# Attention on one core: value bursts of two key tiles side by side, maxima six ahead, and the maxima's turn in the sums' bank

## The reference, cut to what matters

```python
q = (query @ Wq).reshape(b, sq, 32, 32).transpose(0, 2, 1, 3)   # 32 heads of 32
k = (key @ Wk).reshape(b, sk, 8, 32).transpose(0, 2, 1, 3)      # 8 key/value heads, 4 query heads each
v = (value @ Wv).reshape(b, sk, 8, 32).transpose(0, 2, 1, 3)
scores = jnp.einsum('bhqd,bhkd->bhqk', q, jnp.repeat(k, 4, axis=1)) * 32 ** -0.5
probs = jax.nn.softmax(scores, axis=-1)
out = jnp.einsum('bhqk,bhkd->bhqd', probs, jnp.repeat(v, 4, axis=1))
```

## Time and profile before

| | |
|---|---|
| median of 3 runs (lowest to highest) | 915.27 us (914.51 to 922.08) |
| the profiled execution | 919.78 us, span 918.0 us |
| attention, first score of group 0 to the last value burst | 346.7 to 773.9 us of the span |
| PE busy over the span | 846.3 us, 92% |
| DVE, ACT, POOL busy | 591.5, 448.6, 534.0 us |
| costliest groups | reductions 301.0 us (x256), exponentials 279.7 us (x512), scores 179.8 us (x512), items' matmuls 156.3 us (x512), value bursts 137.5 us (x1024) |

### The profile page before, as it was taken

How to read it: one execution, slowest core, us unless ns; L and a number is a source line. 1 busy time by engine, 2 the same in 40 slices (tenths; PEclk the granted TensorE clock), 3 DMA queues, 4 the chain that set the end, 5 groups by cost and what they waited for, 6 DMA issues and landing times.

```text
span 918.0 us, 13982 instructions
## 1 busy us (share of the span) xinstructions
PE 846.3 (92%) x4456; PEld 333.9 (36%) x4456; DVE 591.5 (64%) x846; ACT 448.6 (49%) x741; POOL 534.0 (58%) x235
## 2 busy tenths in 40 slices
PE   3789898969979999999999999999999988999998
PEld 2656564424424442222222222222222212444443
DVE  4657545988836756777876777787877731254621
ACT  4244435645521216666666667677676665021200
POOL 3544125974623334778878888888888788122100
PEclk9799899989989999999999999999999999999999
DMA  6899884322997521554454455445544433222232
GB/s 206 231 211 230 197 216 92 89 84 47 150 229 199 148 73 44 125 124 91 99 105 95 107 123 112 95 100 109 123 93 108 92 69 70 46 48 57 57 126 80
DMA packets 121673, 107.80 MB, mean 117 GB/s; under 512 B 86176, under 2 KB 106656, under 8 KB 117536
## 3 DMA queue, kind: packets, MB, share of 16 engines
q1 hardware_dynamic: 116160, 73.69, 31.8%
q0 software_dynamic: 4608, 33.56, 18.1%
q10 hardware_dynamic: 864, 0.00, 0.0%
HBM read 41.55 MB, written 12.58 MB: 59 GB/s over the span
## 4 chain that ended last, share of the span: by engine, by line
PE 60%; DVE 14%; DMA 7%; issue 7%; SPq 4%; DVEq 4%; ACT 2%; POOLq 1%; POOL 0%; ACTq 0%
PE sbank L1564 10%; PE sbank L1573 10%; PE mpair L1504 9%; DVE mx L1268 5%; DVEq L931 4%; PE sbank L1642 3%; PE sbank L1657 3%; PE sbank L1646 3%; PE sbank L1659 3%; PE sbank L1644 3%; PE sbank L1403 3%; PE sbank L1404 3%; PE sbank L1405 3%; DMA regD<-mT 2%; PE sbank L1583 2%
## 5 line engine op out<-in xcount | busy, mean ns | idle before, releaser
L1268 DVE TENSOR_REDUCE mx<-mpair 128x1 f32<-128x1024 f32 x256 | 301.0, 1215 | 86.6 <-PE mpair L1504 86.4
L873 ACT ACTIVATE regC<-sbank 128x512 f32<-128x512 f32 x512 | 279.7, 595 | 127.3 <-PE sbank L1564 126.6
L1564 PE MATMUL sbank<-regD 98*128 98x512 f16 x512 | 179.8, 388 | 11.9 <-DMA regD<-mT 6.0
L603 POOL TENSOR_TENSOR wraw<-regC 128x2048 f32<-128x2048 f32 x32 | 145.2, 4537 | 25.8 <-ACT regC L873 14.9
L1504 PE MATMUL mpair<-regD 96*128 96x512 f16 x512 | 156.3, 382 | 3.8 <-DVE mT L1278 3.5
L1573 PE MATMUL sbank<-regC,regD 128*32 128x512 f32 x1024 | 137.5, 609 | 1.0 <-ACT regC L873 1.0
L1564 PEld LDWEIGHTS sbank<-regD 98*128 98x128 f16 x512 | 46.3, 97 | 204.6 <-ACT regC L873 164.8
L603 POOL TENSOR_TENSOR regD<-regC 128x2048 f32<-128x2048 f32 x16 | 72.7, 4541 | 27.9 <-ACT regC L873 27.9
L603 POOL TENSOR_TENSOR tail<-regC 128x2048 f32<-128x2048 f32 x16 | 76.7, 4791 | 0.8 <-ACT regC L873 0.8
L1504 PEld LDWEIGHTS mpair<-regD 96*128 96x128 f16 x512 | 49.2, 99 | 55.7 <-DVE mT L1278 10.6
L496 POOL TENSOR_SCALAR xT_lo<-xT_lo,sc 128x1024 f32<-128x1024 f32 x16 | 29.5, 1846 | 65.9 <-DVE X L977 46.9
(11 more groups left out here) (170 smaller groups left out, 1264.9 us busy)
## 6 DMA issues: line engine op xcount, KB each, us to landing
regD<-wraw POOLq DMA_DIRECT2D x16, 1024.0 KB, 7.0
tail<-wraw POOLq DMA_DIRECT2D x16, 1024.0 KB, 7.0
xT_lo<-in_ctx SPq DMA_DIRECT2D x16, 512.0 KB, 5.1
wraw<-in_L_ffn_W_int SPq DMA_DIRECT2D x8, 512.0 KB, 4.4
X<-in_x SPq DMA_DIRECT2D x4, 1024.0 KB, 8.0
wraw<-in_L_xattn_Wq SPq DMA_DIRECT2D x8, 512.0 KB, 3.8
wraw<-in_L_xattn_Wo SPq DMA_DIRECT2D x8, 512.0 KB, 4.5
regD<-q_hi_scratch SPq DMA_DIRECT2D x32, 128.0 KB, 2.4
```

The costliest lines, as they stand in the source:

```text
L603: nc.gpsimd.tensor_tensor(p_sum[pr if pr < 3 else 1][:, :, :], probs[:, (2 * pr) % 4, :, :], probs[:, (2 * pr) % 4 + 1, :, :], ALU.add).th ...
L873: nc.scalar.activation(probs[:, kt % 4, h, :], bank[4 + h % 2], ACT.Exp, scale=SCALE).then_inc(s["exp_ok"], 1)
L1268: v.tensor_reduce(mx[m][:, bass.ds(n, 1)] if par is not None else mx[m][:, n:n + 1], slot[:, :, :], AX.XY, ALU.max).then_inc(s["mx_red"], 1)
L1564: pe.matmul(bank[4 + h % 2], kst[par][0:98, kt * P:(kt + 1) * P], qst[par][0:98, h * 512:(h + 1) * 512], start=True, stop=True).then_inc(s ...
```

## The change

`att` on PE goes through 4 pairs of key tiles, a and b, instead of 8 tiles. Scores 0 and 1 of a pair's first tile stand at the end of the pair before (of the first pair, at its start). Then come the value bursts of both tiles of the pair before, back to back, in pairs 0 and 2 followed by `sum_half`. Behind them, S for a score and M for half of an item: S(a2) M S(a3) M S(b0) M M S(b1) S(b2) M M S(b3) M S(next a0) M S(next a1). So a pair has the same 8 scores and 8 halves of 4 items as two tiles had.

`LEAD` is 6. Pair 0 takes items 6 to 9 of the next group, pair 1 items 10 to 13, pair 2 items 14 and 15 and then 0 and 1 of the group after, pair 3 items 2 to 5. The query projections take two more items (3 + 3 instead of 2 + 2), and the group before the last two fewer. `turn_max` stands directly behind the value bursts of pair 3, and writes into bank 7 instead of bank 2, so nothing in `mpair1` waits for `split_max` any more; it waits instead until bank 7 has been read (`inv_ok`). On DVE `invert`'s second part moves behind item 15, and `split_max` behind the reduction of item 0 of the group after. ACT, POOL and SP keep their instructions and order.

```diff
-        LEAD = 4
+        LEAD = 6
...
-        Q1_ITEMS += [[(0, ITEMS - 1)]] + [[(1, 2 * n), (1, 2 * n + 1)] for n in range(LEAD // 2)]
+        Q1_ITEMS += [[(0, ITEMS - 1)]] + [[(1, 3 * n + i) for i in range(3)] for n in range(LEAD // 3)]
...
                     if not first and n == ITEMS - 3:
                         invert(g - 1, 0)
-                        invert(g - 1, 1)
-                if ahead >= 1:
-                    split_max(g + 1, cur, g // 3 + 1)
+                if not first:
+                    invert(g - 1, 1)
                 for n in range(LEAD):
                     if ahead >= 2:
                         reduce_item(g + 2, far, n)
+                    if n == 0 and ahead >= 1:
+                        split_max(g + 1, cur, g // 3 + 1)
...
             def turn_max(g, par):
                 pe.wait_ge(s["mx_red"], ITEMS * (g + 1))
-                pe.transpose(bank[2][:, 0:P], mx[par][:, :], id32[:, :]).then_inc(s["mt_mm"], 1)
+                if not (isinstance(g, int) and g < 2):
+                    pe.wait_ge(s["inv_ok"], g - 1)
+                pe.transpose(bank[7][:, 0:P], mx[par][:, :], id32[:, :]).then_inc(s["mt_mm"], 1)
...
+                def half_pair(i, half):
+                    if i < len(items):
+                        dg, par, n = items[i]
+                        if half == 0:
+                            pe.wait_ge(s["mx_red"], ITEMS * (g + dg) + n - 1)
+                        max_half(par, n, n % 2, half)
+
+                pe.wait_ge(mrow[cur], 32 * (g // 3 + 1))
+                for j in range(NPAIR):
+                    ka, kb = 2 * j, 2 * j + 1
+                    if j == 0:
+                        score(g, cur, ka, 0, first)
+                        score(g, cur, ka, 1, first)
+                        if not first:
+                            pv(g - 1, far, KT - 2)
+                            pv(g - 1, far, KT - 1)
+                    else:
+                        pv(g, cur, ka - 2, first)
+                        pv(g, cur, ka - 1, first)
+                    if j in (0, 2) and not first:
+                        sum_half(g - 1, j // 2, isinstance(g, int) and g == 1)
+                    if j == 2 and ahead >= 2:
+                        pe.wait_ge(stg[far], 112 * ((g + 2) // 3 + 1))
+                    if j == 3 and ahead >= 1:
+                        turn_max(g + 1, nxt)
+                    items = [todo.pop(0) for _ in range(4) if todo]
+                    score(g, cur, ka, 2, first)
+                    half_pair(0, 0)
+                    score(g, cur, ka, 3, first)
+                    half_pair(0, 1)
+                    score(g, cur, kb, 0, first)
+                    half_pair(1, 0)
+                    half_pair(1, 1)
+                    score(g, cur, kb, 1, first)
+                    score(g, cur, kb, 2, first)
+                    half_pair(2, 0)
+                    half_pair(2, 1)
+                    score(g, cur, kb, 3, first)
+                    half_pair(3, 0)
+                    if j < NPAIR - 1:
+                        score(g, cur, kb + 1, 0, first)
+                    half_pair(3, 1)
+                    if j < NPAIR - 1:
+                        score(g, cur, kb + 1, 1, first)
```

More of the change, by code:

```diff
@@ L1275, in split_max @@
                     dve.wait_ge(mrow[prev], 32 * nth_prev)
-                v.tensor_scalar(mT[0][:, :], bank[2][0:16, 0:P], -1.0 / MROW, None, ALU.mult)
+                v.tensor_scalar(mT[0][:, :], bank[7][0:16, 0:P], -1.0 / MROW, None, ALU.mult)
                 d()
-                v.scalar_tensor_tensor(out=mT[1][:, :], in0=bank[2][0:16, 0:P], scalar=-1.0 / MROW, in1=mT[0][:, :],
+                v.scalar_tensor_tensor(out=mT[1][:, :], in0=bank[7][0:16, 0:P], scalar=-1.0 / MROW, in1=mT[0][:, :],
                                        op0=ALU.mult, op1=ALU.subtract).then_inc(s["mt_cp"], 1)
@@ L1540, in between @@
                     if j == 3 and len(items) > 1:
-                        if items[-1] == (1, 1):
-                            pe.wait_ge(s["mt_cp"], 1)
                         max_scores(*items[-1][:1], *items[-1])
@@ L1591, in att @@
                 todo += [(2, far, n) for n in range(LEAD)] if ahead >= 2 else []
[L1593 to L1596, removed]
-                        turn_max(g + 1, nxt)
[L1598 to L1621, removed]
+                def half_pair(i, half):
[4 more added lines that the diff above has]
+                        max_half(par, n, n % 2, half)
@@ L1634, in _ @@
             att(G - 1, 0, ahead=0)
+            pv(G - 1, 0, KT - 2)
             pv(G - 1, 0, KT - 1)
```

## The result

The changed kernel takes 947.7 us (median of 4 runs, 946.08 to 949.26) against 915.97 before (4 runs): ratio 1.0335, interval 1.03 to 1.0369. Slower by 31.7 us, forecast 29.7.

What follows compares the result with a forecast made beforehand. The prediction took a chain of scores and exponentials through two score banks, 2.88 us a tile, as the bound. Groups and projections summed to +32.2 us, row waits gave -2.5, net +29.7: forecast 945 us, range 930 to 962.

Steps and rivals of the forecast that it cites:

- The bound: Key tiles of the kernel before: a chain through two score banks, 2.88 us a tile, sets the pace, not PE.
- The argument from group 15: Group 15 makes no items, PE has a third less to do, yet its key tile takes 2.89 us.
- the rival that reads PE as the bound: All groups: 24.1 us each, 888 us in all, about 909 if POOL stops it; chance 0.05 for 909, 0.04 lower.
- The plain pair: Pair without sum or turn: its fourth item waits for the second's reduction, so 6.35 us instead of 5.77.
- Pair 3: Pair with turn and split: items wait for reductions behind the split, so it takes 7.45 us.
- The join of two bursts: Between back-to-back value bursts: they join at 0.45 us a pass; a full exit and entry would be 0.87.
- Pairs 0 and 2: Pairs with sum_half behind the bursts: two more passes, 0.91 us, make each 7.26 us.
- A group: The four pairs of a full group: 28.32 us against 26.14, or +2.18, for thirteen groups.
- The small terms: Outside the thirteen full groups: group 0 +1.5, group 14 +1.0, group 15 +0.5, projections +0.9 us.
- POOL's loop: POOL's additions and folds run no faster than about 26.0 us a group (25.97), which fits within 28.3.
- The maxima rows: Row transfers before a group's first score: 3.9 us of room instead of 3.3, shorter PE waits, -2.5 us.
- the third rival: PE's clock in the groups: new waits lower it once a group, about 1.8 us each, +23, 968 us; chance 0.06.

Runs made afterwards that it cites:

- lightened: The kernel before, with exponentials, reductions and POOL's additions covering half their columns: 893.9 us, ratio 0.9756 to the kernel before.
- experiments 1: The changed kernel, each maxima reduction reading only half of its two banks, exponentials' scale 16 times smaller: 928.1 us, ratio 1.0134 to the kernel before.
- 2: The changed kernel, each exponential writing only half of its 512 columns: 940.4 us, ratio 1.0268 to the kernel before.
- 4: The changed kernel, both halves of a pair's first item put ahead of score a3 on PE: 943.6 us, ratio 1.0296 to the kernel before.
- experiment 3: The changed kernel with LEAD = 4 instead of 6 and the split ahead of the reduction of item 0: 931.7 us, ratio 1.0177 to the kernel before.
- kernels of 8: The kernel before, single bursts kept, with LEAD = 6, the turn in bank 7 and tile 6, the split behind two reductions: 919.8 us, ratio 1.0032.
- 9: The single-burst kernel with LEAD = 6, POOL's subtraction moved behind addition 1 and ACT's copy to tile 0: 920.4 us, ratio 1.004 to the kernel before.
- 10: Single bursts, LEAD = 6, POOL's subtraction moved, plus the turn in tile 5 and the split ahead of item 0's reduction: 917.8 us, ratio 1.0016.

## Why the prediction was right

- **The bound.** That tiles of 2.88 us are a chain of scores and exponentials and not PE's work held only by a hair: lightened, a tile with items takes 2.84, while one of group 15, which has none, falls from 2.89 to 2.46. Two bounds lay 0.04 apart. The argument from group 15 was sound, but it hid how close PE was; the rival that reads PE as the bound was wrong about the pairs, not about the tiles.
- **The plain pair**, 6.35 forecast, 6.32 measured, by the chain named (experiments 1, 2 and 4). PE's idle share rose to 8% (25.89 busy of 28.26), less than the 10 and more that were named as a sign.
- **Pair 3**, 7.45 against 7.42, and its cause, the split ahead of needed reductions (experiment 3).
- **The join of two bursts.** Taken at 0.45 a pass. 16 matmuls end 1.92 after the first starts, so three passes take 1.92 less the last one's 0.59, or 0.44 each with the offsets inside a pass; the pass behind the join comes 0.43 after the one ahead of it. Well inside the bound, and six of these account for 0.1 us a group.
- **Pairs 0 and 2**, 7.26 each, measured 7.18 and 7.34. Pair 0 is better by the passes. Pair 2 is worse because ACT's copy of the output stands in it: score b2 waits 0.45 us for ACT there. The forecast had no term for it, and the two misses cancelled.
- **A group**, 28.32 against 28.26.
- **The small terms.** Group 0's pairs took 6.32, 6.33 and 7.27 us and group 15's undisturbed pair 5.90 (forecast 5.93), close to the reckoning. Their totals did not come out: group 0 was forecast at +1.5 and went from 27.39 to 26.68 us between the two traces (the kernel before had a slow clock in it, at 349.9 to 353.3), group 15 at +0.5 and went, from its first score to its last, from 23.9 to 27.8 (two slow pairs). The projections were forecast at +0.9, and the attention began 2.8 later (at 349.6 instead of 346.7; at 347.2 to 349.7 in the kernels of 8, 9 and 10). That such misses make up for each other in part is luck.
- **POOL's loop** of 25.97 us was read rightly as a loop of additions and folds. It is the ring of experiment 9: 25.8 to 25.9 us a group in the kernels of 8 and 9, with no work of PE in it. It decided nothing here, as 28.3 lies above it.
- **The maxima rows.** With more room none of PE's matmuls waited for them, as forecast; the reason given, 0.6 us more room, is only half: the rows are also issued later behind a fold that is nearly through.
- **The clock** was at 1.00 in twelve of groups 1 to 13. It fell twice to its lower level: at 461.0 to 464.4, where two pairs took 0.9 to 1.0 longer than their like, and at 792.1 to 798.9 in group 15, where two pairs took 7.6 and 7.0 us. Ahead of the first the longest wait of PE was 0.99 us (pair 3, behind the split), ahead of the second 0.62.

```profile
458.47 0.60 PE L1505 MATMUL mpair<-regD 96*128 96x512 f16 x2 [0.99 <-DVE mx L1268]
...
791.54 2.38 PE L1565 MATMUL sbank<-regD 98*128 98x512 f16 x4 [0.62 <-ACT regC L873]
```

  By its own sign, a clock under 1.00 without a wait above 2 us, the prediction was wrong here: the third rival's mechanism occurred, twice in the attention and not once a group. And group 15, whose short idles were the argument against that rival, is one of the places. Why it came twice and not once a group no row explains, so that part of the forecast was luck.

## What to carry to other kernels

When a schedule has holes that other engines fill, count what stands between two bursts against the number of buffers, not against the engine's load: DVE was busy three quarters of the time, and four reductions between two bursts with two buffers still set the pace (shorter reductions were tried, more buffers were not). Saving switches on the fullest engine pays only after the chains through its neighbours are shorter than its own work. When a wait is for a small transfer, look which large one was issued before it. The one kernel here that issues the small one first is also the only one, of those that compute everything, that beats the kernel before (by 5.5 us). And before work is taken off a loop, check that it stands in the loop and not in one of its waits.

## What the runs showed of the hardware

- A float32 burst goes on into the next at about 0.43 us per pass of four side-by-side matmuls of 512 columns, with different weights and also into another PSUM bank (in pair 2 `sum_half` starts at 591.94, four passes or 1.74 us behind the value bursts at 590.20). A 16-bit neighbour on either side costs about 0.1: the last score starts 0.31 ahead of the burst (583.57 to 583.88) where two 16-bit matmuls are 0.22 apart, and the next score 0.54 behind the last pass (585.19 to 585.73) where two passes are 0.43 apart.
- Two 4 KB transfers from SP's queue, issued 0.5 to 5 us behind an accumulating transfer of 1 MB from POOL's queue (7.0 us from issue to landing in the median), land with that one, mostly 0.15 to 0.4 us after it, or 2.3 us from the first one's issue to the second one's landing if that is later (the changed kernel: issued at 600.57, behind a fold that ended at 601.7, landed at 602.8): medians 2.4, 3.2 and 5.8 us in three kernels, against 1.7 when issued ahead of it. The Trainium skill (DMA: Bandwidth & Descriptors, "Queues, rings and completion order") says that the write which counts a transfer's semaphore up lands only after every earlier write of the same DMA engine, in whatever queue. By that rule, the trace agrees: what is late is the notice of the rows, at the end of the fold's writes, which were issued first. In experiment 10 the first of the two came up to 2.8 us ahead of the fold's recorded end, so the end of the whole fold is not what every notice waits for. Whether the rows' data themselves land early no run here shows.
